# Sixteen-byte steps between pairs of batches and weight slots, and routed down products cut into six

## The reference, cut to what matters

```python
x = x + L0(x, cond_8)      # per batch: x @ (sum of 8 masked matrices weighted by cond_8) + bias
x = x + L1(x, cond_8)      # base matrix + LoRA of rank 16, experts weighted by cond_8
# L2: two of eight experts per batch (softmax, top 2), and a shared expert for all; width 512
#     w * (gelu(x @ gate) * (x @ up)) @ down, summed over the two experts, plus the shared one
# L3: one of eight experts per batch (argmax); width 256
#     (silu(x @ W_up + b_up) * (x @ W_gate + b_gate)) @ W_down + b_down
```

## Time and profile before

| | us |
|---|---|
| median of the runs | 135.24 |
| the profiled execution's own time | 135.81 |
| its span in the trace | 134.0 |
| PE busy | 129.9 (97% of the span) |
| DVE, ACT, POOL busy | 101.7, 99.0, 75.2 |

### The profile page before, as it was taken

The page is one execution under the profiler, slowest core; times in us unless marked ns, Lnnn a source line. Parts: engine busy times, 40 slices in busy tenths (PEclk is TensorE's granted clock), DMA queues, the critical chain, the costliest instruction groups (busy, mean ns, idle before and its releaser), DMA issues.

```text
span 134.0 us, 3164 instructions
## 1 busy us (share of the span) xinstructions
PE 129.9 (97%) x866; PEld 118.9 (89%) x866; DVE 101.7 (76%) x201; ACT 99.0 (74%) x205; POOL 75.2 (56%) x89
## 2 busy tenths in 40 slices
PE   7999999999999999999999999999999999999990
PEld 5988888888888899999999999999999999999980
DVE  0589898797775777768877687877868677898791
ACT  3774699979946478777797777766767659989860
POOL 0228449979980027468496684963452634426770
PEclk9999999999999999999999999999999999999998
DMA  4999999999005955556765657756577465665224
GB/s 151 329 395 400 415 399 402 397 403 378 19 0 213 373 202 232 237 232 247 313 257 224 248 218 313 286 220 248 220 287 312 191 273 227 259 271 203 72 87 157
DMA packets 11489, 34.54 MB, mean 258 GB/s; under 512 B 1104, under 2 KB 2512, under 8 KB 11472
## 3 DMA queue, kind: packets, MB, share of 16 engines
q1 hardware_dynamic: 11184, 34.15, 65.0%
q10 hardware_dynamic: 288, 0.20, 0.5%
HBM read 12.32 MB, written 1.05 MB: 100 GB/s over the span
## 4 chain that ended last, share of the span: by engine, by line
PE 90%; DVE 3%; ACT 1%; POOL 1%; issue 1%; ACTq 0%; DVEq 0%; POOLq 0%
PE up L298 31%; PE acc L298 30%; PE gate L298 29%; DVE x_res L1003 1%; DVE h_pair L923 1%; DVE up L1012 1%; POOL x_lo L779 1%; POOL x_res L805 1%; ACT h_pair L636 0%; ACTq L224 0%; ACT h_act L689 0%; DVE h_pair L1035 0%; DVE acc L1028 0%; ACT h_pair L709 0%; DVE x_res L1044 0%
## 5 line engine op out<-in xcount | busy, mean ns | idle before, releaser
L773 POOL TENSOR_TENSOR dn_lo<-slabs,dn_hi 128x256 fp32r<-128x256 f32 x40 | 29.7, 742 | 39.6 <-ACT dn_hi L654 39.5
L630 ACT ACTIVATE h_act<-gate 128x512 f32<-128x512 f32 x48 | 28.8, 600 | 23.9 <-PE gate L298 22.6
L923 DVE TENSOR_TENSOR h_pair<-up,h_pair 128x512 fp32r<-128x512 f32 x55 | 37.5, 681 | 0.0
L933 DVE SCALAR_TENSOR_TENSOR up<-h_act,w_route,up 128x512 f32<-128x512 f32 x32 | 24.1, 754 | 15.0 <-PE up L298 14.4
L298 PE MATMUL gate<-x_hi,w_gu 128*128 128x256 f32 x160 | 34.3, 278 | 0.0
L298 PE MATMUL up<-x_hi,w_gu 128*128 128x256 f32 x158 | 33.4, 276 | 0.0
L636 ACT ACTIVATE h_pair<-up 128x512 fp32r<-128x512 f32 x55 | 32.8, 597 | 0.0
L298 PEld LDWEIGHTS gate<-x_hi,w_gu 128*128 128x128 f32 x160 | 27.3, 188 | 0.2
L298 PE MATMUL acc<-h_pair,dn_hi 128*128 128x512 f32 (+1 forms) x76 | 27.2, 373 | 0.0
L298 PEld LDWEIGHTS up<-x_hi,w_gu 128*128 128x128 f32 x158 | 26.8, 188 | 0.0
L298 PE MATMUL gate<-x_lo,w_gu 128*128 128x256 f32 x80 | 22.2, 277 | 0.0
(11 more groups left out here) (128 smaller groups left out, 205.1 us busy)
## 6 DMA issues: line engine op xcount, KB each, us to landing
w_gu<-slabs SPq DMA_DIRECT2D x40, 512.0 KB, 3.0
slabs<-slabs_moe SPq DMA_DIRECT2D x8, 768.0 KB, 13.1
slabs<-slabs_l SPq DMA_DIRECT2D x4, 768.0 KB, 8.5
sh_raw<-slabs_shared SPq DMA_DIRECT2D x2, 384.0 KB, 5.2
x_res<-x_rest SPq DMA_DIRECT2D x1, 768.0 KB, 6.9
outT<-x_res SPq DMA_DIRECT2D x6, 128.0 KB, 1.9
slabs<-second_in SPq DMA_DIRECT2D x1, 320.0 KB, 3.3
slabs<-third_in SPq DMA_DIRECT2D x1, 256.0 KB, 3.8
```

Source lines behind the costliest of these rows:

```text
L630: nc.scalar.activation(h_act[:, u % 2, :], gate_ps[u % 2][:], ACT.Gelu_apprx_tanh).then_inc(act_done, 1)
L773: nc.gpsimd.tensor_tensor(dn_lo[:, q % W_SLOTS, :], slab_cols(at, DOWN_AT, 256), dn_hi[:, q % W_SLOTS, :].bitcast(F32), ALU.subtract).then ...
L923: V.tensor_tensor(h_lo[:, u % H_SLOTS, :], h_of(u), h_hi[:, u % H_SLOTS, :].bitcast(F32), ALU.subtract).then_inc(h_lo_done, 1)
L933: ins = V.scalar_tensor_tensor(h_of(u), h_act[:, k, :], weight, h_of(u), ALU.mult, ALU.mult)
```

## The change

Three edits. First, pair `p` of `x_hi` and of `x_lo` starts 16 bytes (four floats) later than it would have, times `p`; slot `k` of `w_gu` likewise, times `k`. So x of batches 0 and 1 starts at 352 modulo 512, of batches 2 and 3 at 368, then 384 and 400; the slots of `w_gu` start at 416, 432, 448, 464. Both tensors get 512 bytes more, so what follows keeps its remainder; `place_sh` moves ahead of the small tensors. `h_pair`, `dn_hi`, `dn_lo`, `sh_hi` and `sh_lo` keep theirs. Second, `routed_down` becomes a call of `slab_down`: six matmuls of 256 columns. Third, `add_halves` goes; `add_acc` adds one 256-wide accumulator.

```diff
-        x_hi = sb("x_hi", [P, TOKENS], F32R)
-        x_lo = sb("x_lo", [P, TOKENS], F32R)
+        x_hi_all, x_lo_all = (sb(n, [P, TOKENS + 128], F32R) for n in ("x_hi", "x_lo"))
+        x_hi, x_lo = ([x[:, p * (PAIR + 4):p * (PAIR + 4) + PAIR] for p in range(PAIRS)] for x in (x_hi_all, x_lo_all))
+        place_sh = sb("place_sh", [P, 24])
...
-        w_gu = sb("w_gu", [P, W_SLOTS, 2 * SLAB_GU], F32R)
+        w_gu_all = sb("w_gu", [P, W_SLOTS * 2 * SLAB_GU + 128], F32R)
+        w_gu = [w_gu_all[:, k * (2 * SLAB_GU + 4):k * (2 * SLAB_GU + 4) + 2 * SLAB_GU] for k in range(W_SLOTS)]
...
+        def x_of(parts, tok):
+
+            p = tok.start // PAIR
+            return parts[p][:, tok.start - p * PAIR:tok.stop - p * PAIR]
...
             def routed_down(q):
                 b, j = q // 4, q % 4
                 if j == 0:
                     acc_bank_free(PAIRS + b)
-                hidden_split(R0 + q)
-                pe.wait_ge(wd_hi_done, q + 1)
-                pe.wait_ge(wd_lo_done, q + 1)
-                slot = (R0 + q) % H_SLOTS
-
-                def both(c, start, stop):
-                    w, h = slice(c * P, (c + 1) * P), slice(c * S, (c + 1) * S)
-                    return mm(acc(b, 512), dn_hi[:, q % W_SLOTS, w], h_pair[:, slot, :, h], start, stop)
-
-                def low(c):
-                    w, h = slice(c * P, (c + 1) * P), slice(c * S, (c + 1) * S)
-                    mm(acc(b, S), dn_lo[:, q % W_SLOTS, w], h_hi[:, slot, h], False, False)
-
-                both(0, j == 0, False)
-                low(0)
-                low(1)
-                both(1, False, j == 3).then_inc(down_done, 1)
-
+                slab_down(R0 + q, q, acc(b, S), j == 0, j == 3)
...
-            def add_halves(b, down):
-
-                at = slice(b * S, (b + 1) * S)
-                dve.wait_ge(down_done, down)
-                V.tensor_tensor(x_res[:, at], acc(b, 512)[:, S:2 * S], x_res[:, at], ALU.add).then_inc(half_added, 1)
-                dve.wait_ge(half_added, b + 1)
-                V.tensor_tensor(x_res[:, at], acc(b, S), x_res[:, at], ALU.add).then_inc(acc_read, 1)
-
...
-                        add_halves(b - 1, R0 + 4 * b)
+                        add_acc(b - 1, S, R0 + 4 * b)
...
-                    add_halves(B - 1, T0)
+                    add_acc(B - 1, S, T0)
```

More of the change, by code:

```diff
@@ L156, in build @@
         place_h = sb("place_h", [P, 112])
-        h_pair = sb("h_pair", [P, H_SLOTS, 2, 512], F32R)
-        h_hi, h_lo = h_pair[:, :, 0, :], h_pair[:, :, 1, :]
+        h_all = sb("h_pair", [P, H_SLOTS, 2, 512], F32R)
+        h_pair = [h_all[:, k, :, :] for k in range(H_SLOTS)]
+        h_hi, h_lo = [h[:, 0, :] for h in h_pair], [h[:, 1, :] for h in h_pair]
         out_part = sb("out_part", [P, 2, S])
@@ L179, in build @@
         d_shared = [sem("d_shared0"), sem("d_shared1")]
-        d_out, half_added, last_half = sem("d_out"), sem("half_added"), sem("last_half")
+        d_out, last_half = sem("d_out"), sem("last_half")
         dve_step, zeros_ready = sem("dve_step"), sem("zeros_ready")
@@ L280, in _ @@
                 at = slab_of(sp, q)
-                sp.dma_start(w_gu[:, q % W_SLOTS, :].bitcast(F32),
+                sp.dma_start(w_gu[q % W_SLOTS][:].bitcast(F32),
                              slab_cols(at, 0, 2 * SLAB_GU)).then_inc(d_gu[q % W_SLOTS], DMA)
@@ L407, in shared_up @@
                 at = (c // 2) * SLAB + (c % 2) * P
-                tok = bass.ds(p * PAIR, PAIR)
+                tok = slice(p * PAIR, (p + 1) * PAIR)
                 for out, off, done in ((gate_ps[c % 2], 0, gate_ready), (up_ps[c], 256, up_ready)):
                     w = slice(at + off, at + off + P)
-                    split_product(out[:], sh_hi[:, w], sh_lo[:, w], x_hi[:, tok], x_lo[:, tok]).then_inc(done, 1)
+                    split_product(out[:], sh_hi[:, w], sh_lo[:, w], x_of(x_hi, tok), x_of(x_lo, tok)).then_inc(done, 1)
             def first_shared_up():
@@ L418, in first_shared_up @@
                 for out, w, _ in parts:
-                    mm(out[:], sh_hi[:, w], x_hi[:, 0:PAIR], True, False)
+                    mm(out[:], sh_hi[:, w], x_hi[0][:], True, False)
                 pe.wait_ge(sh_lo_ready, 1)
                 for out, w, _ in parts:
-                    mm(out[:], sh_lo[:, w], x_hi[:, 0:PAIR], False, False)
+                    mm(out[:], sh_lo[:, w], x_hi[0][:], False, False)
                 pe.wait_ge(x2_lo, 1)
                 for out, w, done in parts:
-                    mm(out[:], sh_hi[:, w], x_lo[:, 0:PAIR], False, True).then_inc(done, 1)
+                    mm(out[:], sh_hi[:, w], x_lo[0][:], False, True).then_inc(done, 1)
             def hidden_split(u):
@@ L446, in shared_down @@
                 w = slice(at, at + P)
-                split_product(acc(p, 512), sh_hi[:, w], sh_lo[:, w], h_hi[:, c, :], h_lo[:, c, :],
+                split_product(acc(p, 512), sh_hi[:, w], sh_lo[:, w], h_hi[c][:, :], h_lo[c][:, :],
                               c == 0, c == 3).then_inc(down_done, 1)
@@ L456, in gate_up_split @@
                 slot = q % W_SLOTS
-                return (w_gu[:, slot, off:off + P], w_gu[:, slot, SLAB_GU + off:SLAB_GU + off + P])
+                return (w_gu[slot][:, off:off + P], w_gu[slot][:, SLAB_GU + off:SLAB_GU + off + P])
             def slab_up(u, q, b):
@@ L467, in slab_up @@
                         w_hi, w_lo = gate_up_split(q, off + c * P)
-                        last = split_product(out[:, c * S:(c + 1) * S], w_hi, w_lo, x_hi[:, tok], x_lo[:, tok])
+                        last = split_product(out[:, c * S:(c + 1) * S], w_hi, w_lo, x_of(x_hi, tok), x_of(x_lo, tok))
                     last.then_inc(done, 1)
@@ L562, in last_gate_up @@
                         w_hi, w_lo = gate_up_split(q, off + c * P)
-                        split_product(out, w_hi, w_lo, x_hi[:, tok], x_lo[:, tok]).then_inc(done, 1)
+                        split_product(out, w_hi, w_lo, x_of(x_hi, tok), x_of(x_lo, tok)).then_inc(done, 1)
             def last_down():
@@ L612, in round_x2 @@
                 for b in (2 * p, 2 * p + 1):
-                    last = nc.scalar.activation(x_hi[:, b * S:(b + 1) * S], x2_ps(b), ACT.Identity, bias=c_b[:, b:b + 1])
+                    last = nc.scalar.activation(x_of(x_hi, slice(b * S, (b + 1) * S)), x2_ps(b), ACT.Identity, bias=c_b[:, b:b + 1])
                 last.then_inc(x2_hi, 1)
@@ L622, in _ @@
             act.wait_ge(acc_read, ACC_BIAS)
-            nc.scalar.activation(x_hi[:, 0:S], x2_ps(0), ACT.Identity, bias=c_b[:, 0:1]).then_inc(x2_hi_half, 1)
+            nc.scalar.activation(x_hi[0][:, 0:S], x2_ps(0), ACT.Identity, bias=c_b[:, 0:1]).then_inc(x2_hi_half, 1)
             round_shared(1)
@@ L635, in round_h @@
                     act.wait_ge(down_done, u + 1 - H_SLOTS)
-                nc.scalar.activation(h_hi[:, u % H_SLOTS, :], h_of(u), ACT.Copy).then_inc(h_hi_done, 1)
+                nc.scalar.activation(h_hi[u % H_SLOTS][:, :], h_of(u), ACT.Copy).then_inc(h_hi_done, 1)
             def round_expert(e):
@@ L708, in _ @@
                 h = slice(c * S, (c + 1) * S)
-                nc.scalar.activation(h_hi[:, t % 4, h], last_up[c], ACT.Copy).then_inc(h_hi_done, 1)
+                nc.scalar.activation(h_hi[t % 4][:, h], last_up[c], ACT.Copy).then_inc(h_hi_done, 1)
             add_bias(4)
@@ L895, in _ @@
             dve.wait_ge(x2_first_sum, 2)
-            V.tensor_scalar(x_hi[:, S:2 * S], x2_ps(1), c_b[:, 1:2], None, ALU.add).then_inc(x2_hi, 1)
+            V.tensor_scalar(x_hi[0][:, S:], x2_ps(1), c_b[:, 1:2], None, ALU.add).then_inc(x2_hi, 1)
             def split_x2(p):
@@ L902, in split_x2 @@
                     at = slice(b * S, (b + 1) * S)
-                    last = V.scalar_tensor_tensor(x_lo[:, at], x2_ps(b), c_b[:, b:b + 1], x_hi[:, at].bitcast(F32),
+                    last = V.scalar_tensor_tensor(x_of(x_lo, at), x2_ps(b), c_b[:, b:b + 1], x_of(x_hi, at).bitcast(F32),
                                                   ALU.add, ALU.subtract)
@@ L922, in lo_h @@
                 dve.wait_ge(h_hi_done, u + 1)
-                V.tensor_tensor(h_lo[:, u % H_SLOTS, :], h_of(u),
-                                h_hi[:, u % H_SLOTS, :].bitcast(F32), ALU.subtract).then_inc(h_lo_done, 1)
+                V.tensor_tensor(h_lo[u % H_SLOTS][:, :], h_of(u),
+                                h_hi[u % H_SLOTS][:, :].bitcast(F32), ALU.subtract).then_inc(h_lo_done, 1)
             def product(u, weight=None):
@@ L953, in round_x3 @@
                 at = slice(b * S, (b + 1) * S)
-                V.tensor_copy(x_hi[:, at], x_res[:, at]).then_inc(x3_hi, 1)
+                V.tensor_copy(x_of(x_hi, at), x_res[:, at]).then_inc(x3_hi, 1)
             def weigh():
```

9 lines of the change are left out of this document (4 added, 5 removed).

## The result

The changed kernel takes 137.34 us (median of 4 runs, 137.27 to 137.95) against 135.24 before: a ratio of 1.0156, 95% interval 1.0131 to 1.018, so slower by 2.1 us. The forecast was 134.4. Its profiled execution takes 137.27 us with a span of 135.5.

A forecast was written before the change was run, and what follows sets the result against it. PE's matmul stream was taken as the bound. Profiled 135.81 - 0.86 (Part 1; Parts 2 and 3 at 0) = 134.95, runs 0.57 lower: 134.38, forecast 134.4 us; range 133.6 to 136.4, its own 134.1 to 134.9.

The forecast's parts named there:

- What bounds the kernel: Whole kernel: PE's matmul stream sets its length, busy 97% of the span; only the distance between matmul starts counts.
- Part 1: Routed down products: six matmuls of 256 for four bring units from 2.066 to 2.04 us, saving 0.86 us.
- Part 2: DVE: one add for two removes 3.3 us of its work beside PE's stream; nothing worth counting on the path.
- The cover of the transfers: DMA into w_gu slots: issued 6.05 us before use, takes 3.0 us, 4.6 at most; cover 3.0, worst case 1.4.
- Part 3: New starts of x and weights: distances 16 to 112 in 30 units, shared 0 to -16p; cost taken as 0.
- Rival B: Shifted units: new distances bring x-products to 118 ns at 256 columns; in full 136.4 us; chance 0.22.
- the upper bound: Cost of new distances: 30 units x 0.05 = 1.5 us, plus 72 x 7 ns = 0.5; +2.0 us.
- a B that also spoils matmuls with old distances: Cost beyond Rival B's full price of 136.4 us; shares about 0.06 above the range with another rival.
- (D): Shifted units: new distances help, starts under 113 ns; range reaches to a gain of 0.8, 133.6 us; chance 0.12.

The follow-up runs named there:

- six_only: Changed kernel with both 16-byte steps set to 0, keeping the six narrow down products and single add; ratio 0.9949 to the kernel before.
- dist_low: As six_only, but the four w_gu slots start 0, 16, 32 and 48 bytes behind the remainder of x; 137.17 us, one run, beside 135.72 before.
- sh_64: As six_only, but sh_hi and sh_lo start 64 bytes behind the remainder of x and h instead of 0; ratio 1.0243, 138.28 us.
- both_16: As six_only, but all of x and all w_gu slots start 16 bytes later; 136.87 us, one run, beside 135.72 before.
- x_only: Changed kernel with the 16-byte step of x alone, all w_gu slots at one remainder; ratio 1.0182 to the kernel before.
- w_only: Changed kernel with the 16-byte step of w_gu alone, x and the shared stage as before; ratio 1.0156 to the kernel before.
- h_16: As six_only, but h and the down weights start 16 bytes later; ratio 1.0103.
- dist_128: As six_only, but the w_gu slots start 64, 192, 320 and 448 bytes behind the remainder of x; 134.29 us, one run, beside 135.72 before.
- step_128: Changed kernel with steps of 128 bytes instead of 16 between pairs of x and between slots of w_gu; ratio 1.0105.
- sh_64_cut1: As sh_64, but the last of three shared down products in the routed stage is six 256-column matmuls; ratio 1.0009 or 1.0015 (assignment not stated), 3 us under sh_64.
- all_16: As six_only, but all fp32r operands (x, h, w_gu, dn, shared weights) start 16 bytes later; ratio 1.0005.
- moving_128: As six_only, but x and h both start 128 bytes later, weights as they were; ratio 1.0243, two runs, 137.56 and 139.02 us.

## Why the prediction was wrong

**What bounds the kernel** was right. PE is the chain: pieces of PE alone, without idle in the 64.06 us of the routed stretch, and busy for 131.3 of 135.5 us in the changed kernel, and what the starts lose shows in the time.

**Part 1** was right in its working: units at 2.04 in all of the routed stage behind the first three. The sum of 0.86 stands in the stream of `six_only`; the runs give 0.7 (0.4 to 1.0). **Part 2** was right about the path, on which nothing moved; DVE's busy time fell from 101.7 to 98.9 us, by 2.8 where 3.3 were reckoned. The cover of the transfers held as well: the longest took 5.1 us.

**Part 3 is the step that failed**: its term was put at 0 by "A pace that is the same at 0 and at 64 is most likely the same at 16 to 112." The two good places of before belong to two widths, 0 to the wide products and 64 to the narrow ones, and the pace isn't the same at both: narrow products take 2.04 us a unit at 64 and 2.14 at 0 (`dist_low`). Wide ones take 2.04 at 0 and 2.10 at 64 (`sh_64`), though for them the place isn't shown to be the cause. I read two points of two curves as one flat one. The new distances, which no row of before had, cost 2.8 us.

Rival B had the right sign and, in the main, the right mechanism, and a price of 2.0, set as the upper bound. By the unrounded starts of the changed kernel and of `six_only`, the routed and L3 stages lose 2.10 us in the x products, where the bound had 1.5, and 0.73 us in the down products, where it had nothing; the shared stage loses 0.48, where it had 0.5. In the stream that is 3.3 us together. From the last x product to the last instruction of DVE the changed kernel is 0.3 us shorter, which leaves 3.0, and the runs give 2.8. Two terms were too small. The pace of 118 ns was taken as the slowest there is, since the earlier trace rows had no other, and its price of 0.05 us a unit was a difference of rounded starts (0.056 unrounded). The x products of the 30 shifted units run at 119 ns on average, 122 in the slowest unit, which is 0.067 us a unit. And the down products lose too, though their own addresses are the old ones: they come behind a switch (`both_16`) or in a stream that is still slow (`x_only`); the bound held that only matmuls with a new address of their own lose. In the text I named the second case, "a B that also spoils matmuls with old distances", and gave it part of 6% without a price.

The first routed unit of before, 118 ns at unchanged addresses, I took as evidence for B. By its pace it is rather the slower of the two states: entered behind the wide shared products, left with the next wide ones. Its own cost is 0.05 us. The same pace in `sh_64` costs 3. So B had the right sign partly by luck: its main evidence was of another effect.

Moving the start of the weights alone takes a unit from 2.04 to 2.13 us (`w_only`), where I forecast nothing. How the two starts act on each other, no run shows.

(D), that the new distances help and shifted units run below 113 ns a matmul, fell: no run shows a narrow fp32r stream below that. So the gain of up to 0.8 us to which the range reached into D is shown by no run; the steps cost 2.8. The records of plain fp32, 379 ns for 256 columns, gave no hint of what fp32r does.

## What to carry to other kernels

In this kernel, where matmuls in fp32r run back to back, the start addresses of weights and moving operand are a parameter worth 2% (2.8 us between the changed kernel and `six_only`). Once a layout runs at the plain pace, keep its relations: weights against moving operand (up to 0.09 us a unit of 2.04 in `w_only`), and the operands of one product against those of the next (0.04 in `both_16` and `h_16`). In these runs `w_gu` could be padded by multiples of 128 bytes (`dist_128`) and x by 256 (pair 2 of `step_128`) without a loss in the steady stream (2.04 us a unit in both). Read the time between matmul starts, not their lengths (in the slowest unit above a record is 0.28 or 0.29 us long, where the earlier trace rows have 0.28), and compare units with equal columns; a pace a few per cent over the plain one through a whole stage may have been fixed by the last few matmuls before it, as in `sh_64` (2.12 us a unit, 36 units long, against 2.04 in `sh_64_cut1`). A bound built from the slowest row at hand isn't an upper bound when the change makes a situation that no row has.

## What the runs showed that I had not expected

- A good distance of stationary and moving operand for 256-wide fp32r products with a period of 128 bytes and a narrow place: 2.04 us a unit at 64, 192, 320 and 448, 2.12 at 60, 2.10 at 72 (one run each).
- Two paces of the same narrow stream at the same addresses, 113.3 and 117.8 ns (2.04 and 2.12 us a unit), each kept for the 36 units to the end of the stream; a few matmuls at the entry choose, for 3 us.
- Mixed widths disturb, at either distance: the two wide matmuls in a routed unit of before, at 64, cost 0.026 us; the three in the second and third routed unit of `six_only`, at 0, cost 0.020. Cutting the first kind is a gain of 0.7 us, though it adds 64 matmuls and as many loads of weights (`six_only`).
- No whole unit of any run is faster than 2.04 us, the plain pace that the kernel before already had: 113.3 ns for 256 columns and 226.7 for 512, at a granted clock of 1.00. Nothing that was moved or cut took the fp32r stream below.

What stays open: why the distance matters at all; whether wide products go by distance (`sh_64`), by the remainder itself (`all_16`) or by a state; whether a switch costs by the moving operands or by the weights; and whether `moving_128` is slow by its addresses or by its state. No run tried to find a state from which a stream at another distance is fast.
